# Two more steps of lag in a windowed-attention pipeline, and a second PSUM buffer in a mixture-of-experts stage

## The chip, the cores and the metric

The kernel runs on the 8 cores of one Trainium2 chip. Each core computes 2048 of the 16384 tokens, with its own copy of all weights. The metric is the device time in microseconds of the slowest core.

## What is computed

One transformer layer, cut to its core:

```python
# x: [16384, 1024]; every block ends with layernorm(x + block(x))
q, k, v = split(x @ qkv_w + qkv_b)              # 16 heads of 64
s = (q / 8) @ k.T                               # local window: the 128 keys before a query
local = softmax(where(0 < dist <= 128, s, -1e9)) @ v
pooled = x.reshape(64, 256, 1024).mean(1)       # 64 latent tokens over ALL 16384 tokens
rk, rv = split(pooled @ rkv_w)
remote = softmax(where(chunk_allowed, (x @ rq_w) @ rk.T / 8, -1e9)) @ rv @ rout_w
gate = sigmoid(local @ gl_w + remote @ gr_w)
x = layernorm(x + (gate*local + (1-gate)*remote) @ out_w)
# FFN: shared part plus 16 experts, the 4 chosen ones weighted by `combine`
shared = (silu(x @ sgw.T) * (x @ suw.T)) @ sdw.T
for e in range(16):                             # dense: all tokens through all experts
    h = silu(x @ gate_w[e]) * (x @ up_w[e])     # [tokens, 256]
    routed += (h * combine[:, e]) @ down_w[e]
x = layernorm(x + shared + routed)
```

## The kernel before

The program is a row of blocks (phases 0, 1, 15, 2, 3). Inside a block each engine has its own queue, in the order in which the Python code calls `P.op`; an engine works its queue strictly in order. `waits` are semaphore values of other engines, and `P.drain("ve")` stands between dependent VectorE operations. The blocks follow one another with a barrier.

**Phase 0** works through the core's 2048 tokens in four chunks of 512. For each chunk: TensorE transposes the tokens (L334, through `transpose_group`), ScalarE copies them out (`xfm`, L341), then follow the q, k, v and rq projections (L350, through `proj`), then `emit_pool(8)`, then the attention loop. A group is one pair of heads and 128 queries; there are G = 32 groups in a chunk, 128 in all. A group passes six stages:

- `stA`: TensorE scores into `ps_sc` (L494). It waits for the newest `stB`.
- `stB`: VectorE adds the mask (two operations, L511) into `maskedb`, takes the row maximum (L519) and clamps it (L523). `maskedb` has two buffers; it waits for `stC` of the group two before.
- `stC`: ScalarE exponentials (two operations with a sum, L538) into `p_b`, two buffers.
- `stD`: VectorE adds an epsilon to the sum (L553), inverts it (L558) and scales the row (two operations, L565) into `pn_b`, two buffers.
- `stE`: TensorE transposes the four 128x128 parts (L581) into one of two `ps_bt`; ScalarE copies them to `pT_b` (L591).
- `stG`: TensorE multiplies with v (four matmuls, L611) into one of two `ps_pr`; ScalarE casts the result into `local_sb` (L622).

After every eighth group TensorE gets six tiles of the pooling of all 16384 tokens (`emit_pool(6)`, L319, 12 matmuls), whose loads (`ring`) are issued on the GpSimd queue. At the end of a chunk SyncE stores `local_sb`. The next chunk's transposes use the same `ps_bt` slots, and stand behind the loop in TensorE's queue. After the last chunk the pooled tokens are evacuated, transposed and projected, and the block ends with the store of `local_sb`.

**Phase 2** runs the experts: 8 token blocks of 256, 16 experts each, 128 steps. In TensorE's order a step is: the combine weights of this expert broadcast to 128 partitions (`ps_wb`, L1442, one matmul), 16 gate matmuls into `ps_g` (L1453), 16 up matmuls into `ps_u` (L1466), and the 8 down matmuls of the previous expert into `ps_rt` (L1489), which collect over the 16 experts. ScalarE applies Silu to `ps_g` (L1504). VectorE multiplies it with `ps_u` (`h_sb`, L1508) and that with `ps_wb` (`hwst`, L1518). The up matmuls wait for the load of `uwb` and for the previous expert's `h_sb`. Loads: `uwb` on SyncE's queue, `dwb` on GpSimd's, four buffers each. At the end of a token block VectorE adds the residual (`ry`, L1536), with a load of `y1r` and a store per half on SyncE's queue, ahead of the next block's `uwb` loads.

PSUM in phase 2: `ps_rt` two tiles of 1024 f32 columns, `ps_g` and `ps_u` one of 512 each, `ps_wb` two of 256.

Of the kernel before, what the change touches and what calls it, by code (L numbers as in the profile page):

```python
# [7 lines left out]
F32 = mybir.dt.float32  # L8
# [103 lines left out]
class Builder:  # L112
# [88 lines left out]
    def phase0(self):  # L201
        nc, d, sm = self.nc, self.d, self.sem
        pe, pp, ve, se = (sm[k] for k in ("pe", "pp", "ve", "se"))
        c0 = ExitStack()
        S = lambda n, s, t: c0.enter_context(nc.sbuf_tensor(n, s, t))
        PS = lambda n, s, t: c0.enter_context(nc.psum_tensor(n, s, t))
# [36 lines left out]
        P = Plan()  # L243
# [27 lines left out]
        for dst, src in [(self.maskAB[:], d["maskAB_in"]),  # L271
# [14 lines left out]
             waits=[self.tk_consts], inc=se)  # L286
# [79 lines left out]
        for c in range(self.p0_nch):  # L366
# [14 lines left out]
            if c + 1 < NCH:  # L381
                ld_own[c + 1] = st_xo.dma(
                    P, "ge", xown[:], R3(d["x_own"][(c + 1) * 512:(c + 2) * 512, :]),
                    waits=[(pe, tr_pe)])
# [241 lines left out]

            ST = self.p0_st
            if self.p0_attn:
                for i in range(G + 3):
                    if 1 <= i <= G and ST >= 2:  # L630
                        stB(i - 1)
                    if i < G:
                        stA(i)
                    if 1 <= i <= G and ST >= 3:
                        stC(i - 1)
                    if 2 <= i <= G + 1 and ST >= 4:
                        stD(i - 2)
                    if 2 <= i <= G + 1 and ST >= 5:
                        stE(i - 2)
                    if 3 <= i <= G + 2 and ST >= 6:  # L640
                        stG(i - 3)
                    if i < G and i % 8 == 7:
                        emit_pool(6)

# [723 lines left out]
    def phase2(self):  # L1368
# [12 lines left out]
        ry = S("ry", [128, 2, 1024], F32)  # L1381
        ps_rt = [PS(f"ps_rt{i}", [128, 1024], F32) for i in range(2)]
        ps_g = PS("ps_g2", [128, 512], F32)
        ps_u = PS("ps_u2", [128, 512], F32)
        ps_wb = [PS(f"ps_wb{i}", [128, 256], F32) for i in range(2)]

        P = Plan()
        st_y1s = self.new_stream("y1s2", 4)
# [7 lines left out]
        y1r_rel = [None, None]  # L1396
        ry_rel = [None, None]
        wb_rel = [None, None]
        rt_rel = [None, None]
        silu_prev = 0  # L1400
        h_prev = 0
# [17 lines left out]
        for tb in range(8):  # L1419
# [8 lines left out]
            for e_i in range(17):  # L1428
                if e_i < 16:
                    su = e_i % 4  # L1430
                    wu = [uwb_rel[su]] if uwb_rel[su] is not None else []
                    uwld[e_i] = st_uw.dma(P, "sy", uwb[:, su],
                                          d["uwbf_sp"][e_i],
                                          waits=wu + self.tk_precast_ud)
                    wd = [dwb_rel[su]] if dwb_rel[su] is not None else []
                    dwld[e_i] = st_dw.dma(P, "ge", dwb[:, su], d["dwbf_sp"][e_i],
                                          waits=wd + self.tk_precast_ud)
                    sw = e_i % 2
                    if self.p2_mode >= 1:
                        ww = [wb_rel[sw]] if wb_rel[sw] is not None else []  # L1440
                        ww += [(se, self._p15_comb_se), self.tk_gec]
                        P.op("te", lambda e, sw=sw, e_i=e_i, tb=tb: e.matmul(  # L1442
                            ps_wb[sw][:], self.ue16[:, e_i * 128:(e_i + 1) * 128],
                            self.combT[0:16, tb * 256:(tb + 1) * 256],
                            start=True, stop=True), waits=ww, inc=pe)
                    vwb = pe.n
                    if self.p2_mode < 2:
                        continue
                    wg = [self.tk_gw, ldy_a, ldy_b, (se, silu_prev)]
                    for mh in range(2):  # L1450
                        for cc in range(8):
                            P.op("te", lambda e, e_i=e_i, cc=cc, mh=mh, sl=sl:
                                 e.matmul(ps_g[:, mh * 256:(mh + 1) * 256],  # L1453
                                          self.gw_sb[:, e_i, cc,
                                                     mh * 128:(mh + 1) * 128],
                                          y1s[:, sl, cc, :],
                                          start=(cc == 0), stop=(cc == 7)),
                                 waits=wg if (cc == 0 and mh == 0) else (),
                                 inc=pe if (cc == 7 and mh == 1) else None)
                            wg = ()  # L1460
                    vg = pe.n
                    wu2 = [uwld[e_i], (ve, h_prev)]
                    for mh in range(2):
                        for cc in range(8):
                            P.op("te", lambda e, su=su, cc=cc, mh=mh, sl=sl:
                                 e.matmul(ps_u[:, mh * 256:(mh + 1) * 256],  # L1466
                                          uwb[:, su, cc, mh * 128:(mh + 1) * 128],
                                          y1s[:, sl, cc, :],
                                          start=(cc == 0), stop=(cc == 7)),
                                 waits=wu2 if (cc == 0 and mh == 0) else (),  # L1470
                                 inc=pe if (cc == 7 and mh == 1) else None)
                            wu2 = ()
                    vu = pe.n
                    uwb_rel[su] = (pe, pe.n)
# [27 lines left out]
                if e_i < 16:  # L1502
                    sgsl = e_i % 2
                    P.op("se", lambda e, sgsl=sgsl: e.activation(  # L1504
                        out=sg_sb[:, sgsl, :], in_=ps_g[:], func=AF.Silu),
                        waits=[(pe, vg), (ve, h_prev2[sgsl])], inc=se)
                    silu_prev = se.n
                    P.op("ve", lambda e, sgsl=sgsl: e.tensor_tensor(  # L1508
                        out=h_sb[:], in0=sg_sb[:, sgsl, :], in1=ps_u[:],
                        op=OP.mult),  # L1510
                        waits=[(se, silu_prev), (pe, vu)], inc=ve)
                    h_prev = ve.n
                    h_prev2[sgsl] = ve.n
                    P.drain("ve")
                    sw = e_i % 2
                    wb3 = ps_wb[sw][:].unsqueeze(1).broadcast_to([128, 2, 256])
                    whw = [(pe, prev_down_pe)]
                    P.op("ve", lambda e, e_i=e_i, wb3=wb3: e.tensor_tensor(  # L1518
                        out=hwst[:, e_i % 2, :].rearrange("p (n m) -> p n m", n=2),
                        in0=h_sb[:].rearrange("p (n m) -> p n m", n=2),  # L1520
                        in1=wb3, op=OP.mult), waits=whw, inc=ve)
                    hw_ve[e_i] = ve.n
                    wb_rel[sw] = (ve, ve.n)
                    P.drain("ve")
                    prev_down_pe = down_pe[e_i - 1] if e_i >= 1 else prev_down_pe
# [391 lines left out]
```

How the kernel before makes its waits and increments, by code:

```python
        def run(e, fn=fn, w=tuple(w), inc=inc, incn=incn):  # L66
            for (s, v) in w:
                e.wait_ge(s.h, v)
            ins = fn(e)
            if inc is not None:
                ins.then_inc(inc.h, incn)
```

## Time and profile before

| | us |
|---|---|
| median of the two runs shown | 2845.77 |
| lowest and highest of them | 2769.34, 2922.2 |
| profiled execution | 2742.85 |
| its span, slowest core (core 4) | 2741.3 |
| spans of the eight cores | 2712.7 to 2741.3 |

Over the span TensorE is busy 62%, its weight loads 39%, VectorE 30%, ScalarE 23%, GpSimd 7%. These are averages over stages with different limits: phase 0 takes about the first 696 us, phases 1 and 15 run to about 1396, the experts to about 2265, and the shared part to the end. A stretch's limit is read from the order of time inside it: the engine whose queue has no gap but those it makes itself.

### The profile page before, as it was taken

The page shows a single profiled execution, that of the slowest core. Times are in us where ns is not written, and L with a number is a line of the kernel's source. Part 1 is how long each engine was busy: PE and PEld are TensorE (multiplying, and loading weights), DVE is VectorE, ACT ScalarE, POOL GpSimd, SP SyncE. Part 2 cuts the span into 40 slices and gives each one's busy share as a digit, 9 for nine tenths or more (in the row PEclk, how much of TensorE's full clock was granted, in tenths as well). Part 3 has the DMA queues.
Part 4 walks back from the last instruction along what each step waited for, and adds up shares of the span by engine and source line. Part 5 has one row for each costly group of instructions (what it writes and reads, how often), then busy time and mean ns, then how long its engine had stood idle before and what let it go on. Part 6 is the DMA issues. An engine that isn't in the chain of part 4 may idle for free. (4 is left out here: it accounts for less than half of the span.)

```text
span 2741.3 us, 33324 instructions; the slowest of 8 cores (2712.7 to 2741.3 us)
## 1 busy us (share of the span) xinstructions
PE 1712.0 (62%) x11255; PEld 1055.7 (39%) x11368; DVE 819.1 (30%) x2083; ACT 642.6 (23%) x1693; POOL 201.9 (7%) x329
## 2 busy tenths in 40 slices
PE   0858677685345442000249779779779783877886
PEld 0423233332111110000136557557556553655654
DVE  0173645638344441001232222222222220222222
ACT  1264554636312220002611001001000000122212
POOL 1100100000011111110001000000000000000000
PEclk9968777686666666555569899889899896998998
DMA  9644553523977777656735655555555546122112
GB/s 169 100 70 73 72 83 54 78 39 55 151 164 177 153 169 145 137 130 171 210 130 170 198 182 175 191 181 185 177 179 196 171 139 215 55 77 85 55 62 77
DMA packets 185652, 363.15 MB, mean 132 GB/s; under 512 B 30272, under 2 KB 89984, under 8 KB 183952
## 3 DMA queue, kind: packets, MB, share of 16 engines
q0 software_dynamic: 94048, 182.90, 32.9%
q1 hardware_dynamic: 91440, 178.11, 20.3%
q8 instruction: 96, 1.57, 0.2%
q14 instruction: 68, 0.56, 0.1%
HBM read 367.69 MB, written 79.69 MB: 163 GB/s over the span
## 5 line engine op out<-in xcount | busy, mean ns | idle before, releaser
L1466 PE MATMUL ps_u<-y1s,uwb 128*128 128x256 bf16 x2048 | 257.5, 281 | 114.8 <-DMA uwb<-uwbf_sp 114.8
L1508 DVE TENSOR_TENSOR h_sb<-sg_sb,ps_u 128x512 bf16<-128x512 bf16 x128 | 88.0, 688 | 585.5 <-PE ps_u L1466 585.5
L1466 PEld LDWEIGHTS ps_u<-y1s,uwb 128*128 128x128 bf16 x2048 | 205.5, 101 | 146.0 <-issue 117.0
L1453 PE MATMUL ps_g<-y1s,gw_sb 128*128 128x256 bf16 x2048 | 250.7, 277 | 9.9 <-DMA y1s<-y1fm_sp 9.9
L1504 ACT ACTIVATE sg_sb<-ps_g 128x512 bf16<-128x512 f32 x128 | 76.4, 597 | 759.6 <-PE ps_g L1453 759.6
L1489 PE MATMUL ps_rt<-dwb,hwst 128*128 128x512 bf16 x960 | 228.1, 379 | 4.5 <-DVE hwst L1518 0.5
L1636 PE MATMUL ps_g<-y1s,sgw 128*128 128x256 bf16 x1024 | 144.5, 288 | 114.5 <-ACT sgs L1652 61.1
L1453 PEld LDWEIGHTS ps_g<-y1s,gw_sb 128*128 128x128 bf16 x2048 | 192.1, 99 | 48.9 <-issue 11.7
L1170 PE MATMUL ps_b<-ident,y1bf 128*128 128x128 bf16 x128 | 16.2, 306 | 277.7 <-ACT y1bf L1150 229.1
L1636 PEld LDWEIGHTS ps_g<-y1s,sgw 128*128 128x128 bf16 x1024 | 104.7, 103 | 134.6 <-issue 116.7
L538 ACT ACTIVATE p_b<-maskedb,mn_sb 128x256 bf16<-128x256 f32 x256 | 127.9, 500 | 58.0 <-DVE mn_sb L523 58.0
L1645 PE MATMUL ps_u<-y1s,suw 128*128 128x256 bf16 x1024 | 140.6, 283 | 0.0
L1489 PEld LDWEIGHTS ps_rt<-dwb,hwst 128*128 128x128 bf16 x1024 | 99.5, 98 | 98.3 <-issue 4.9
L45 POOL DMA_DIRECT2D dwb<-dwbf_sp x128 | 67.6, 529 | 896.6 <-PE ps_wb L1442 730.7
L1657 DVE TENSOR_TENSOR h_sb<-sgs,ps_u 128x256 bf16<-128x256 bf16 x128 | 53.3, 421 | 237.0 <-PE ps_u L1645 166.2
L350 PE MATMUL ps_pr<-xfm,qkvw 128*128 128x512 bf16 x500 | 117.7, 397 | 6.1 <-ACT xfm L341 5.4
L1170 PEld LDWEIGHTS ps_b<-ident,y1bf 128*128 128x128 bf16 x128 | 12.4, 137 | 279.1 <-issue 279.1
L1675 PE MATMUL ps_d<-sdw,h_sb 128*128 128x512 bf16 x496 | 109.6, 379 | 8.0 <-DVE h_sb L1657 7.5
L1645 PEld LDWEIGHTS ps_u<-y1s,suw 128*128 128x128 bf16 x1024 | 104.5, 102 | 16.1
L511 DVE TENSOR_TENSOR maskedb<-ps_sc,maskAB 128x256 f32<-128x256 f32 x240 | 90.1, 418 | 55.7 <-PE ps_sc L494 55.5
L581 PE MATMUL ps_bt<-ident,pn_b 128*128 128x128 bf16 x512 | 68.8, 281 | 60.5 <-DVE pn_b L565 60.5
L591 ACT COPY pT_b<-ps_bt 128x512 bf16<-128x512 bf16 x128 | 75.0, 586 | 105.0 <-PE ps_bt L581 105.0
(181 smaller groups left out, 2020.8 us busy)
## 6 DMA issues: line engine op xcount, KB each, us to landing
dwb<-dwbf_sp POOLq DMA_DIRECT2D x128, 512.0 KB, 4.0
uwb<-uwbf_sp SPq DMA_DIRECT2D x128, 512.0 KB, 3.9
ring<-x_all POOLq DMA_DIRECT2D x64, 512.0 KB, 10.2
xres<-x_own SPq DMA_DIRECT2D x16, 512.0 KB, 17.2
gw_sb<-gate_w POOLq DMA_DIRECT2D x4, 2048.0 KB, 40.1
stg<-down_w POOLq DMA_DIRECT2D x16, 512.0 KB, 6.4
y_sp<-y0b SPq DMA_DIRECT2D x16, 512.0 KB, 5.8
dwbf_sp<-stg POOLq DMA_DIRECT2D x16, 512.0 KB, 3.0
```

The lines of the kernel that those rows point to most:

```text
L350: P.op("te", lambda e, sl=slot, kk=kk, nc2=ncols, nr=nrows: e.matmul(ps_pr[sl][0:nr, 0:nc2], lhs_fn(kk), rhs_fn(kk), start=(kk == 0), stop ...
L511: e.tensor_tensor(out=maskedb[:, mb, hh * 256:(hh + 1) * 256], in0=ps_sc[hh][:, mb * 256:mb * 256 + 256], in1=m, op=OP.add),
L538: P.op("se", lambda e, mb=mb, hh=hh, f=f: e.activation(out=p_b[:, mb, hh * 256:(hh + 1) * 256], in_=maskedb[:, mb, hh * 256:(hh + 1) * 256 ...
L591: P.op("se", lambda e, sl=slot, mb=mb: e.copy(out=pT_b[:, mb, :], in_=ps_bt[sl][:]), waits=wv, inc=se)
L1453: e.matmul(ps_g[:, mh * 256:(mh + 1) * 256], self.gw_sb[:, e_i, cc, mh * 128:(mh + 1) * 128], y1s[:, sl, cc, :], start=(cc == 0), stop=(cc ...
L1466: e.matmul(ps_u[:, mh * 256:(mh + 1) * 256], uwb[:, su, cc, mh * 128:(mh + 1) * 128], y1s[:, sl, cc, :], start=(cc == 0), stop=(cc == 7)),
L1489: nh=nh, first=first, last=last: e.matmul(ps_rt[mt][:, nh * 512:(nh + 1) * 512], hwst[:, ep % 2, kc * 256 + mt * 128: kc * 256 + mt * 128 ...
L1504: P.op("se", lambda e, sgsl=sgsl: e.activation(out=sg_sb[:, sgsl, :], in_=ps_g[:], func=AF.Silu), waits=[(pe, vg), (ve, h_prev2[sgsl])], i ...
L1508: P.op("ve", lambda e, sgsl=sgsl: e.tensor_tensor(out=h_sb[:], in0=sg_sb[:, sgsl, :], in1=ps_u[:], op=OP.mult), waits=[(se, silu_prev), (p ...
L1636: P.op("te", lambda e, sl2=slg, mh=mh, cc=cc, sl=sl: e.matmul(ps_g[sl2][:, 0:256], sgw[:, cc, mh * 128:(mh + 1) * 128], y1s[:, sl, cc, :], ...
L1645: P.op("te", lambda e, sl2=slu, mh=mh, cc=cc, sl=sl: e.matmul(ps_u[sl2][:, 0:256], suw[:, cc, mh * 128:(mh + 1) * 128], y1s[:, sl, cc, :], ...
L1675: last=last, sld=sld: e.matmul(ps_d[sld][:, nh * 512:(nh + 1) * 512], h_sb[:, kc, mt * 128:(mt + 1) * 128], sdw[:, kc, nh * 512:(nh + 1) * ...
```

## The change

Two independent edits.

In the attention loop the stages from `stC` on are issued later: exponentials of group i-2 instead of i-1 in step i, normalisation of i-3 instead of i-2, transposes of i-4 instead of i-2, value products of i-5 instead of i-3. The loop has two more steps to finish. No stage's own code changes; no buffer is added.

In phase 2 `ps_u` gets a second buffer, used in turn, so that the up matmuls wait for the product of two experts before instead of the previous one. The PSUM for it comes from `ps_wb`, which has one buffer now. A new ScalarE copy, ahead of the Silu in ScalarE's queue, brings `ps_wb` into `wb_sb` in SBUF (f32, two buffers), and VectorE's second product reads it there. The next `ps_wb` matmul waits for that copy; the copy waits for the second product of two experts before.

```diff
-                for i in range(G + 3):
+                for i in range(G + 5):
                     if 1 <= i <= G and ST >= 2:
                         stB(i - 1)
                     if i < G:
                         stA(i)
-                    if 1 <= i <= G and ST >= 3:
-                        stC(i - 1)
-                    if 2 <= i <= G + 1 and ST >= 4:
-                        stD(i - 2)
-                    if 2 <= i <= G + 1 and ST >= 5:
-                        stE(i - 2)
-                    if 3 <= i <= G + 2 and ST >= 6:
-                        stG(i - 3)
+                    if 2 <= i <= G + 1 and ST >= 3:
+                        stC(i - 2)
+                    if 3 <= i <= G + 2 and ST >= 4:
+                        stD(i - 3)
+                    if 4 <= i <= G + 3 and ST >= 5:
+                        stE(i - 4)
+                    if 5 <= i <= G + 4 and ST >= 6:
+                        stG(i - 5)
                     if i < G and i % 8 == 7:
                         emit_pool(6)
...
-        ps_u = PS("ps_u2", [128, 512], F32)
-        ps_wb = [PS(f"ps_wb{i}", [128, 256], F32) for i in range(2)]
+        ps_u = [PS(f"ps_u2{i}", [128, 512], F32) for i in range(2)]
+        ps_wb = PS("ps_wb", [128, 256], F32)
+        wb_sb = S("wb_sb", [128, 2, 256], F32)
...
-                        ww = [wb_rel[sw]] if wb_rel[sw] is not None else []
-                        ww += [(se, self._p15_comb_se), self.tk_gec]
+                        ww = [(se, self._p15_comb_se), self.tk_gec]
+                        if wb_ps_rel[0] is not None:
+                            ww.append(wb_ps_rel[0])
...
+                        vwb = pe.n
+                        wwc = [(pe, vwb)]
+                        if wb_rel[sw] is not None:
+                            wwc.append(wb_rel[sw])
+                        P.op("se", lambda e, sw=sw: e.copy(
+                            out=wb_sb[:, sw, :], in_=ps_wb[:]), waits=wwc,
+                            inc=se)
+                        wb_ps_rel[0] = (se, se.n)
...
-                    wu2 = [uwld[e_i], (ve, h_prev)]
+                    su2 = e_i % 2
+                    wu2 = [uwld[e_i]]
+                    if psu_rel[su2] is not None:
+                        wu2.append(psu_rel[su2])
...
+                    psu_rel[su2] = (ve, ve.n)
...
-                    wb3 = ps_wb[sw][:].unsqueeze(1).broadcast_to([128, 2, 256])
-                    whw = [(pe, prev_down_pe)]
+                    wb3 = wb_sb[:, sw, :].unsqueeze(1).broadcast_to([128, 2, 256])
+                    whw = [(pe, prev_down_pe), (se, silu_prev)]
```

## Rows read from the trace of the kernel before

**Rows 1.** Busy by stretch (attention; experts): length, PE, PEld, DVE, ACT, POOL, clock, DMA.

```profile
130.47:226.80 96.33, 54.69 (x366) 26.60 (x365) 73.58 (x256) 57.40 (x187) 8.42 (x13) 0.61 0.51 72
1396.30:2265.00 868.70, 726.79 (x5184) 508.84 (x5248) 195.57 (x272) 77.70 (x129) 67.62 (x128) 0.92 0.55 180
```

**Rows 2.** Order of time, one attention group: start us, us, engine, line, operation, [idle before].

```profile
188.88 0.51 ACT L538 ACTIVATE p_b<-maskedb,mn_sb 128x256 bf16<-128x256 f32 x1 [0.18 <-DVE mn_sb L523]
188.94 0.40 PE L494 MATMUL ps_sc<-k_sb,q_sb 64*128 64x256 bf16 x2 [0.72 <-DVE mn_sb L523]
...
189.21 0.48 DVE L565 TENSOR_SCALAR pn_b<-p_b,rvv 128x256 bf16<-128x256 bf16 x2
...
189.61 0.75 DVE L511 TENSOR_TENSOR maskedb<-ps_sc,maskAB 128x256 f32<-128x256 f32 x2
189.79 0.19 ACT L538 ACTIVATION_READ_ACCUMULATOR p_b<-maskedb,mn_sb 128x1 f32 x1
...
189.84 0.59 PE L581 MATMUL ps_bt<-ident,pn_b 128*128 128x128 bf16 x4 [0.51 <-DVE pn_b L565]
...
190.43 0.69 DVE L519 TENSOR_REDUCE mn_sb<-maskedb 128x2 f32<-128x512 f32 x1
190.52 0.58 ACT L591 COPY pT_b<-ps_bt 128x512 bf16<-128x512 bf16 x1 [0.54 <-PE ps_bt L581]
...
191.19 0.17 DVE L523 TENSOR_SCALAR mn_sb<-mn_sb 128x2 f32<-128x2 f32 x1
...
191.51 0.40 PE L494 MATMUL ps_sc<-k_sb,q_sb 64*128 64x256 bf16 x2 [0.72 <-DVE mn_sb L523]
```

**Rows 3.** Waits of the whole run: who waited for whom, us in total, times, longest.

```profile
DVE maskedb L511 <- PE ps_sc L494: 62.6, 20, 6.6
```

**Rows 4.** Order of time in the expert stage, one expert.

```profile
1445.56 0.69 DVE L1508 TENSOR_TENSOR h_sb<-sg_sb,ps_u 128x512 bf16<-128x512 bf16 x1 [4.07 <-PE ps_u L1466]
1446.34 0.69 DVE L1518 TENSOR_TENSOR hwst<-h_sb,ps_wb 128x512 bf16<-128x512 bf16 x1
...
1447.11 0.28 PE L1442 MATMUL ps_wb<-combT,ue 16*128 16x256 bf16 x1
...
1449.08 1.91 PE L1466 MATMUL ps_u<-y1s,uwb 128*128 128x256 bf16 x16
...
1451.10 0.69 DVE L1508 TENSOR_TENSOR h_sb<-sg_sb,ps_u 128x512 bf16<-128x512 bf16 x1 [4.07 <-PE ps_u L1466]
```

**Rows 5.** Waits of TensorE in the expert stage, 1420 to 2240 us.

```profile
PE ps_u L1466 <- DMA uwb<-uwbf_sp: 109.9, 7, 16.7
```

**Rows 6.** Order of time on VectorE at the start of the first chunk's loop.

```profile
130.87 0.76 DVE L511 TENSOR_TENSOR maskedb<-ps_sc,maskA0B 128x256 f32<-128x256 f32 x2 [6.56 <-PE ps_sc L494]
133.18 0.76 DVE L511 TENSOR_TENSOR maskedb<-ps_sc,maskA0B 128x256 f32<-128x256 f32 x2 [0.55 <-PE ps_sc L494]
135.77 0.75 DVE L511 TENSOR_TENSOR maskedb<-ps_sc,maskA0B 128x256 f32<-128x256 f32 x2
```

**Rows 7.** Order of time at the end of the first chunk's loop.

```profile
222.45 4.41 PE L319 MATMUL ps_pool<-ring,zpool 128*64 128x512 bf16 x12
...
227.29 0.58 ACT L591 COPY pT_b<-ps_bt 128x512 bf16<-128x512 bf16 x1 [2.85 <-PE ps_bt L581]
...
227.77 0.27 ACT L622 CAST local_sb<-ps_pr 128x128 bf16<-128x128 f32 x1
227.93 0.60 ACT L591 COPY pT_b<-ps_bt 128x512 bf16<-128x512 bf16 x1
...
228.67 0.31 PE L611 MATMUL ps_pr<-pT_b,v_sb 128*64 128x128 bf16 x4 [0.35 <-ACT pT_b L591]
228.91 0.62 PE L334 MATMUL ps_bt<-ident,xown 128*128 128x128 bf16 x8
```

**Rows 8.** Groups of instructions by line and shape: busy, mean ns, idle before.

```profile
L1504 ACT ACTIVATE sg_sb<-ps_g 128x512 bf16<-128x512 f32 x128 | 76.4, 597 | 759.6 <-PE ps_g L1453 759.6
...
L974 DVE TENSOR_TENSOR d_bf<-localre,remote 128x512 bf16<-128x512 bf16 x32 | 13.6, 426 | 47.8 <-PE ps_g L968 43.3 <-issue 4.5
```

More of the change, by code:

```diff
@@ L1398, in phase2 @@
         wb_rel = [None, None]
+        wb_ps_rel = [None]
+        psu_rel = [None, None]
         rt_rel = [None, None]
@@ L1439, in phase2 @@
                     if self.p2_mode >= 1:
-                        ww = [wb_rel[sw]] if wb_rel[sw] is not None else []
-                        ww += [(se, self._p15_comb_se), self.tk_gec]
-                        P.op("te", lambda e, sw=sw, e_i=e_i, tb=tb: e.matmul(
-                            ps_wb[sw][:], self.ue16[:, e_i * 128:(e_i + 1) * 128],
+                        ww = [(se, self._p15_comb_se), self.tk_gec]
+                        if wb_ps_rel[0] is not None:
+                            ww.append(wb_ps_rel[0])
+                        P.op("te", lambda e, e_i=e_i, tb=tb: e.matmul(
+                            ps_wb[:], self.ue16[:, e_i * 128:(e_i + 1) * 128],
                             self.combT[0:16, tb * 256:(tb + 1) * 256],
                             start=True, stop=True), waits=ww, inc=pe)
-                    vwb = pe.n
+                        vwb = pe.n
[6 more added lines that the diff above has]
+                        wb_ps_rel[0] = (se, se.n)
                     if self.p2_mode < 2:
@@ L1461, in phase2 @@
                     vg = pe.n
-                    wu2 = [uwld[e_i], (ve, h_prev)]
+                    su2 = e_i % 2
+                    wu2 = [uwld[e_i]]
+                    if psu_rel[su2] is not None:
+                        wu2.append(psu_rel[su2])
                     for mh in range(2):
                         for cc in range(8):
-                            P.op("te", lambda e, su=su, cc=cc, mh=mh, sl=sl:
-                                 e.matmul(ps_u[:, mh * 256:(mh + 1) * 256],
+                            P.op("te", lambda e, su=su, su2=su2, cc=cc, mh=mh,
+                                 sl=sl:
+                                 e.matmul(ps_u[su2][:, mh * 256:(mh + 1) * 256],
                                           uwb[:, su, cc, mh * 128:(mh + 1) * 128],
@@ L1507, in phase2 @@
                     silu_prev = se.n
-                    P.op("ve", lambda e, sgsl=sgsl: e.tensor_tensor(
-                        out=h_sb[:], in0=sg_sb[:, sgsl, :], in1=ps_u[:],
+                    P.op("ve", lambda e, sgsl=sgsl, su2=su2: e.tensor_tensor(
+                        out=h_sb[:], in0=sg_sb[:, sgsl, :], in1=ps_u[su2][:],
                         op=OP.mult),
```

## The prediction

> **What bounds the kernel now.** I read the spans of the cores first (2712.7 to 2741.3 us, clocks 0.787 to 0.791: no core stands out), then busy time by stretch, then the order of time inside the two stretches that the diff touches, then the waits. The two edits lie in an attention loop of 32 groups that runs four times, 96.33 us in the first chunk, and in the expert stage, 868.70 us [rows 1].
>
> In the attention stretch no engine looks full: VectorE 73.58 of 96.33 us, ScalarE 57.40, TensorE 54.69 at a granted clock of 0.61, the lower level for most of it. The order of time says more [rows 2]. TensorE's scores (L494) start at 188.94 and again at 191.51, so a group takes 2.57 us. In it VectorE runs without a break: normalisation (L565) 189.21 to 189.69, mask adds (L511) 189.61 to 190.36, row maximum (L519) 190.43 to 191.12, clamp (L523) 191.19 to 191.36, and then the small operations of the next normalisation. The gaps of 0.07 us follow its own drains. None of its rows shows idle time before it. So VectorE's queue sets the 2.57 us; TensorE and ScalarE wait for it, and their idle time there costs nothing. VectorE itself waits where pooling matmuls (L319) stand ahead of the next scores, and at the start of a chunk: 20 times in the whole run, 62.6 us [rows 3].
>
> In the expert stage the order of time shows TensorE as the bound [rows 4]: the `ps_wb` matmul starts at 1447.11 and the up matmuls at 1449.08, with only the 16 gate matmuls between them, and weight loads and matmuls together leave little of the stage free. VectorE's read of `ps_u` (L1508) runs 1445.56 to 1446.25, and the next write of `ps_u` starts at 1449.08. In the waits of 820 us of this stage the longest of TensorE's is 109.9 us for `uwb` loads, seven times at a block boundary, and there is none for VectorE on `ps_u` [rows 5].
>
> **Attention: what the new order moves.** Today step i issues mask+max(i-1), scores(i), exp(i-1), normalise(i-2), transpose(i-2), value product(i-3). Afterwards the last four are exp(i-2), normalise(i-3), transpose(i-4), value product(i-5). Counts of instructions, tiles and DMAs stay; 32 groups end two steps later.
>
> Steady state: VectorE has the same eight operations per group, and none waited for data that now comes earlier. scores(i) still waits for mask+max(i-1), the newest VectorE result, and mask+max(i) still waits for scores(i): 188.94 to 189.61, hidden under the normalisation, as before. I cost the steady state at 0. Its bound on the good side is the drain gaps: period 2.57 less VectorE's durations (0.75+0.69+0.17+0.17+0.17+0.48 = 2.43, two of the 0.17 being the normalisation's small steps, sized as the clamp) is 0.14 us, 18 us over 128 groups.
>
> Fill: normalisation starts one step later, so one more step runs without it. Such a step took 2.31 us (130.87, [0.55] us idle, 133.18), a step with it 2.59 (133.18 to 135.77) [rows 6]: 0.28 us gained per chunk.
>
> Tail: now it counts, since the next chunk's transposes queue behind it on TensorE and ScalarE. Before, the last pooling block ends at 222.45+4.41 = 226.86; two transposes and three value products are left behind it, and the next chunk's transposes start at 228.91, 2.05 us later [rows 7]. Afterwards four transposes and five value products are left, and exp(31) too, because ScalarE's queue has the copy of transpose(28) ahead of it, which waits for the pooling block. Counting from the block's end with steps from rows: first copy starts at 0.43 (227.29); cast 0.48 later, 0.91; exp(31) 0.16 later (227.77 to 227.93), 1.07, and lasts 1.10 (188.88 to 189.98 [rows 2]), 2.17; copy(29) to 2.75; its value product on TensorE ends at about 3.1 (0.31). Meanwhile VectorE normalises 31 after exp(31), 0.17+0.17+0.48 with gaps, 0.97 us (2.57 less 1.60 for adds to clamp), done near 3.2. transpose(31) starts at 3.3 and its copy 0.5 later, 3.8; from a last copy to the last value product 0.74 (227.93 to 228.67) and on to the next transposes 0.24: 4.8. Less 2.05: 2.75 us per chunk. The fourth chunk's tail delays the pooled projections and the spill that phase 1 waits for, by about as much. Sum: 4 x (2.75 - 0.28) = 9.9 us, taken as +10. Bounds: +4, if ScalarE's work packs better (0.48+0.16 us for each of two extra pairs, less the fill, 1.0 per chunk); +16, if exp(31), copies and normalisation run strictly one after another (four copies 0.58, five casts 0.27, exp 1.10, normalisation 0.97, 5.7 us, plus the 0.43 and 0.24, less 2.05, is 4.3 per chunk).
>
> **Experts: a second `ps_u`, `ps_wb` copied out.** The wait taken off TensorE, up(e+1) on h(e), had been met 2.83 us before it was reached (1446.25 against 1449.08) [rows 4]: 0 us. If it had just been uncovered it would be worth up to one VectorE read, 0.69.
> The Trainium skill, "Perfetto Trace Analysis", section Matmuls, says that independent matmul groups should rotate through different PSUM banks so that one's evacuation overlaps the next one's matmuls. By that rule alone the 88 us of rival (e) would come back; the trace disagrees, since the gate, down and `ps_wb` matmuls already lie between two uses of `ps_u`.
>
> Added are 128 ScalarE copies of 128x256 f32. The trace has none; the nearest are the cast of 128x128 at 0.27 us and the Silu of 128x512 at 0.60 [rows 7, 8], so 0.27 to 0.60 and I take 0.43, 35 to 77 us in all. ScalarE is busy 77.70 of 868.70 us there [rows 1]. Behind a copy on its queue stands silu(e), which waits for gate(e) and so for 1.9 us longer than the copy's source. The new wait, `ps_wb`(e+1) on copy(e), has a period of 5.54 us (1445.56+5.54 is the next h) to be met; it costs 0. Without that cover it would be 0.43 x 128 = 55 us. The product `hwst` (L1518, 0.69) now reads SBUF: between the all-SBUF bf16 add's 0.43 [rows 8] and, on the bad side, 0.26 more than now; it lies off the path except before the last down matmuls of a block, eight times, so -2 to +2 us, taken as 0. SP's and POOL's queues issue the same loads on the same waits.
> The Trainium skill, "VectorE: DVE Perf Modes", section Rules for kernel authors, says to accept the slower PSUM read, or copy to SBUF first if many operations follow. One operation reads `wb_sb`, so the rule speaks against the edit; the idle ScalarE makes it cost nothing, and the sum is the same.
>
> **The sum** is made on the profiled execution: 2742.85 + 10 + 0 = 2753 us. The median of the two runs shown is 2845.77 (2769.34 and 2922.2), 3.8% above the profiled time; I forecast on the profiled time's scale.
>
> **Rivals.** (a) *Only the tail grows*: 2753. For it: no idle time on VectorE and TensorE to recover. Chance 0.66.
> (b) *The tail lets TensorE's clock fall before the next projection.* Four transposes take 0.59 at the low level [rows 2] and half of 0.62 for eight at the start of the next chunk [rows 7]; eight such groups in four chunks are 32 x 0.28 = 9 us more: 2762. Against: the clock in the attention stretch is low already. Chance 0.12.
> (c) *VectorE's gaps shrink* because its semaphore waits are all met early: -18+10, 2735. Against: the gaps follow drains. Chance 0.08.
> (d) *The two-deep buffers bind.* exp(i-1) frees `maskedb` for mask(i+1). It now runs after copy(i-4) and cast(i-5), which follow scores(i): 188.94 + 0.40 + 0.68 + 0.48 + 0.27 + 1.10 = 191.87 [rows 2, 7], and VectorE wants the buffer at 189.61+2.57 = 192.18. Before, exp ended at 189.98; the slack falls from 2.2 to 0.3 us. The loop spans two groups, so every 0.1 us beyond the slack costs 0.05 us x 128 = 6 us. A chain 1.3 us longer than these rows say gives 128 x 0.5 = 64 us: 2817. It is the mechanism on the slower side, and passes 2% from a chain 1.15 us longer. Chance 0.08, most of it over 2%.
> (e) *The waits paid off after all*, because VectorE no longer stands still behind the pooling blocks (all of the 62.6 us of [rows 3]: 2753 - 63 = 2690), or because the read of `ps_u` really lay open in every expert (128 x 0.69 = 88: 2665). Against: the scores behind a pooling block keep their place in TensorE's queue, and TensorE never waited for VectorE on `ps_u` [rows 5]. Chance 0.04, most of it over 2%.
> (f) *`ps_wb`'s single buffer stops TensorE* each expert: 2753 + 55 = 2808. Against: 5 us of slack. Chance 0.02.
>
> **How the numbers follow.** Likeliest 2753; its own bounds give 2743 to 2765 (+4-2 and +16+2, with half a per mille for repeat runs). The range takes in (b) and (c) and reaches up to (d) and (f), and covers that the lowest timed run lies 27 us above the profiled one: 2735 to 2820. What a measurement of this kernel can tell from no change is about 2%, 55 us: faster 0.03 (most of (e)), slower 0.08 (most of (d), and (f), which lies at the bound), same 0.89.
>
> **What would show it.** Right: scores of neighbouring groups still 2.57 us apart; the time from the last pooling block's end to the next chunk's transposes near 4.8 instead of 2.05; ScalarE's `wb_sb` copies near 0.43 us and no TensorE wait for them; the expert period still 5.54. Wrong: a period of groups below 2.5 (c) or above 2.65 with VectorE waiting for ScalarE at L511 (d); an expert period that moves; or VectorE's wait behind the pooling blocks shrinking (e).

## The result, and the profile after

The changed kernel takes 2753.37 us (median of 43 runs, 2743.6 the lowest). The kernel before, run beside it, takes 2743.18 us (42 runs, 2730.95 the lowest). The ratio is 1.0036, 95% interval 1.0025 to 1.0047: slower by about 10 us, which is within 2% and yet far outside the uncertainty of so many runs. The median of two runs shown ahead of the prediction, 2845.77 us, was 3.7% above what more runs give for the same kernel. Some executions of either kernel run a few per cent longer with the cores of one die at a lower clock; the ratio leaves them out, as by its size it does the 2922.2 us shown there.

Span and mean granted TensorE clock of the slowest core in the profiled execution after (the others take 2725.8 to 2745.8 us; before 2712.7 to 2741.3):

```profile
core 7: 2750.5 us, clock 0.783
```

One steady attention group of the changed kernel, in order of time (start us, us, engine, line, operation, [idle before it and what ended it]); it answers to [rows 2]:

```profile
188.67 0.17 DVE L523 TENSOR_SCALAR mn_sb<-mn_sb 128x2 f32<-128x2 f32 x1
...
188.98 0.17 DVE L558 RECIPROCAL rvv<-rvv 128x2 f32<-128x2 f32 x1
188.99 0.40 PE L494 MATMUL ps_sc<-k_sb,q_sb 64*128 64x256 bf16 x2 [1.31 <-DVE mn_sb L523]
189.29 0.48 DVE L565 TENSOR_SCALAR pn_b<-p_b,rvv 128x256 bf16<-128x256 bf16 x2
...
189.69 0.75 DVE L511 TENSOR_TENSOR maskedb<-ps_sc,maskAB 128x256 f32<-128x256 f32 x2
...
191.59 0.40 PE L494 MATMUL ps_sc<-k_sb,q_sb 64*128 64x256 bf16 x2 [1.31 <-DVE mn_sb L523]
```

VectorE still works without a break, and TensorE and ScalarE still wait for it. But the scores are now 2.60 us apart (188.99 to 191.59), not 2.57, and between the reciprocal's end (188.98+0.17 = 189.15) and the scaling (189.29) lie 0.14 us, where the kernel before has 0.07.

The end of the first chunk, answering to [rows 7]:

```profile
222.13 4.70 PE L319 MATMUL ps_pool<-ring,zpool 128*64 128x512 bf16 x12
...
227.25 0.59 ACT L591 COPY pT_b<-ps_bt 128x512 bf16<-128x512 bf16 x1 [3.43 <-PE ps_bt L581]
227.27 0.48 DVE L565 TENSOR_SCALAR pn_b<-p_b,rvv 128x256 bf16<-128x256 bf16 x2 [2.50 <-PE ps_bt L581]
...
227.89 0.52 ACT L538 ACTIVATE p_b<-maskedb,mn_sb 128x256 bf16<-128x256 f32 x1
...
229.10 0.17 DVE L553 TENSOR_SCALAR rvv<-ssum 128x2 f32<-128x2 f32 x1 [1.35 <-ACT p_b L538]
...
229.65 0.48 DVE L565 TENSOR_SCALAR pn_b<-p_b,rvv 128x256 bf16<-128x256 bf16 x2
...
230.76 0.59 ACT L591 COPY pT_b<-ps_bt 128x512 bf16<-128x512 bf16 x1 [0.47 <-PE ps_bt L581]
...
231.49 0.30 PE L611 MATMUL ps_pr<-pT_b,v_sb 128*64 128x128 bf16 x4 [0.59 <-ACT pT_b L591]
231.72 0.62 PE L334 MATMUL ps_bt<-ident,xown 128*128 128x128 bf16 x8
```

The last pooling block ends at 222.13+4.70 = 226.83, and the next chunk's transposes start at 231.72. This stretch, called the tail below, takes 4.89 us, against 2.05. The chain is the one of the prediction: copy(28) at 227.25, exp(31) at 227.89, its end lets VectorE invert the sum at 229.10, scaling at 229.65, transpose, copy at 230.76, value product at 231.49.

The expert stage after: the groups of the new copy, the second product and the up matmuls (count | busy us, mean ns of one | idle before and what ended it):

```profile
L1454 ACT COPY wb_sb<-ps_wb 128x256 f32<-128x256 f32 x128 | 47.8, 373 | 530.4 <-PE ps_wb L1446 530.4
L1534 DVE TENSOR_TENSOR hwst<-h_sb,wb_sb 128x512 bf16<-128x512 bf16 x128 | 88.6, 692 | 12.1 <-issue 0.4
L1481 PE MATMUL ps_u<-y1s,uwb 128*128 128x256 bf16 x2048 | 257.2, 281 | 117.1 <-DMA uwb<-uwbf_sp 117.1
```

The 128 copies take 0.37 us each, `hwst` takes 0.69 us as before, the expert period is still 5.54 us (`h_sb` at 1456.35 and 1461.89), and TensorE waits there for the same thing as before, the `uwb` loads (117.1 us over the whole stage, against 114.8 before; [rows 5] has 109.9 of them).

From the first scores of a chunk to the next transposes (in the fourth chunk: to those of the pooled tokens), called the loop below, the slowest cores take:

| us | chunk 1 | 2 | 3 | 4 |
|---|---|---|---|---|
| before (core 4) | 98.44 | 96.55 | 96.69 | 96.50 |
| after (core 7) | 101.06 | 99.45 | 99.32 | 99.23 |

The sum is 10.9 us more. From the transposes to the next chunk's first scores it is 57.03 before and 57.6 after, three times: 1.8 us more. The transposes of the pooled tokens, which follow the fourth loop, so start 12.9 us later (702.64 against 689.73), and the first expert matmul 11.6 us later (1407.87 against 1396.28). One core against another carries some chance with it; averaged over the eight cores these two delays are 12.6 and 11.3 us, and the spans are 10.6 us longer. What lies between the two points takes a little over 1 us back.

### The profile page after: what moved, and what is told of

Same layout as the page of the kernel before. It is cut to its first block and busy times, and to the rows that moved or that the text cites. A ratio compares the mean times of both kernels' runs of the same rounds, so it can differ in the third digit from the quotient of the medians.

```text
span 2750.5 us, 33823 instructions; the slowest of 8 cores (2725.8 to 2750.5 us)
## 1 busy us (share of the span) xinstructions
PE 1721.7 (63%) x11368; PEld 1056.6 (38%) x11368; DVE 814.8 (30%) x2083; ACT 680.8 (25%) x1821; POOL 201.8 (7%) x329
## 5 line engine op out<-in xcount | busy, mean ns | idle before, releaser
L1481 PE MATMUL ps_u<-y1s,uwb 128*128 128x256 bf16 x2048 | 257.2, 281 | 117.1 <-DMA uwb<-uwbf_sp 117.1
L1504 PE MATMUL ps_rt<-dwb,hwst 128*128 128x512 bf16 x1024 | 241.9, 379 | 1.1 <-issue 0.5
L1454 ACT COPY wb_sb<-ps_wb 128x256 f32<-128x256 f32 x128 | 47.8, 373 | 530.4 <-PE ps_wb L1446 530.4
L494 PE MATMUL ps_sc<-k_sb,q_sb 64*128 64x256 bf16 (+1 forms) x256 | 44.4, 330 | 121.5 <-DVE mn_sb L523 121.5
```

Of the source, the lines that this page charges most:

```text
L1481: e.matmul(ps_u[su2][:, mh * 256:(mh + 1) * 256], uwb[:, su, cc, mh * 128:(mh + 1) * 128], y1s[:, sl, cc, :], start=(cc == 0), stop=(cc == ...
L1504: nh=nh, first=first, last=last: e.matmul(ps_rt[mt][:, nh * 512:(nh + 1) * 512], hwst[:, ep % 2, kc * 256 + mt * 128: kc * 256 + mt * 128 ...
```

## The experiments

**Each edit alone.** The first kernel has only the loop's new order, the second only the second `ps_u` with the `wb_sb` copy.

```diff
 # attention only: kernel before, with
-                for i in range(G + 3):
+                for i in range(G + 5):
 ...                                       # and the later stC, stD, stE, stG
 # experts only: the changed kernel, with
-                for i in range(G + 5):
+                for i in range(G + 3):
 ...                                       # and the old order
```

> Only the attention loop's new order; the expert stage as before. Theory (the whole loss lies in the loop's tail and its clock): ratio to the kernel before 1.0036, about +10 us; last pooling block to the next chunk's transposes 4.9 us instead of 2.05, group period 2.60. Rival (the expert edit shares in the loss): ratio 1.001 to 1.002.

> Only the second ps_u and the copied ps_wb; the attention loop as before. Theory: ratio 1.000 within 0.001, expert period 5.54 us, TensorE never waiting for the copy. Rival (the expert edit pays, but the attention edit hides it): ratio 0.998 or less. Rival (it costs): 1.002 or more.

The attention edit alone gave 1.0043 (1.0016 to 1.0071): loops of 100.5, 99.4, 99.3 and 99.2 us on its slowest core, tail 4.89. The expert edit alone gave 1.0005 (0.9983 to 1.0027): loops as before, tail 2.05. So the loss comes from the loop's order; what the expert edit costs or brings is too small for these runs, less than 0.3% either way.

**What lengthened the steady group.** `P.op`, the helper that puts an operation into an engine's queue, leaves out a wait when the engine has already waited for that value of the semaphore or a later one. Before, normalise(g) asks for transpose(g-2), and VectorE had already waited for the scores that were issued after it: the wait was dropped. Afterwards transpose(g-2) is issued after scores(g+2), the newest that VectorE has waited for, so the wait stays in the program. It is met long before it is reached: in the changed kernel the transposes of 186.71 end at 187.32, and the scaling that waits for them starts at 189.29. A third `pn_b` buffer makes normalise(g) ask for transpose(g-3), and the wait is dropped again:

```diff
-        pn_b = S("pn_b", [128, 2, 512], BF16)
+        pn_b = S("pn_b", [128, 3, 512], BF16)
-        rel_pn = [None, None]
+        rel_pn = [None, None, None]
 ...                                       # pn_b and rel_pn indexed by g % 3
```

> The changed kernel with three buffers for the normalised rows pn_b instead of two, so that normalise(g) waits for the transposes of g-3, not g-2. Theory: the 0.03 us by which the group period grew (2.575 to 2.605) is the semaphore wait that normalise(g) now has on transpose(g-2), which is issued after the scores that VectorE has waited for already; with three buffers the period returns to 2.575 and about 3 us come back, ratio to before 1.0025; the tail stays at 4.9 us, since exp(31) sets it and not normalise(30), which waits for the pooling block in the changed kernel. Rival (the period grew for another reason, such as operand traffic of ScalarE): period stays at 2.605. Rival (normalise(30) behind the pooling block sets the tail): tail falls to about 4 us.

The order of time in this kernel:

```profile
187.53 0.17 DVE L558 RECIPROCAL rvv<-rvv 128x2 f32<-128x2 f32 x1
187.53 0.40 PE L494 MATMUL ps_sc<-k_sb,q_sb 64*128 64x256 bf16 x2 [1.25 <-DVE mn_sb L523]
187.78 0.48 DVE L565 TENSOR_SCALAR pn_b<-p_b,rvv 128x256 bf16<-128x256 bf16 x2
...
190.07 0.40 PE L494 MATMUL ps_sc<-k_sb,q_sb 64*128 64x256 bf16 x2 [1.25 <-DVE mn_sb L523]
```

The gap ahead of the scaling is back to 0.08 us (187.70 to 187.78), and the group takes 2.54 us. It is even shorter than before the change, because with the longer lag the wait of normalise(g) on exp(g) is dropped too: VectorE has already waited for exp(g) in order to reuse `maskedb`. The kernel as a whole did not follow: 1.0052 (1.0034 to 1.0070), where 1.0025 was expected. The pooling matmuls show where the gain went; the groups of L319 in phase 0, before, after and with three buffers (mean ns of one is the last number before the second bar):

```profile
L319 PE MATMUL ps_pool<-ring,zpool 128*64 128x512 bf16 x243 | 79.9, 498 | 0.0
```

```profile
L319 PE MATMUL ps_pool<-ring,zpool 128*64 128x512 bf16 x244 | 86.6, 528 | 0.0
```

```profile
L319 PE MATMUL ps_pool<-ring,zpool 128*64 128x512 bf16 x252 | 93.3, 547 | 0.0
```

The program has 256 of them (some records are missing). They are the same instructions; the granted clock of TensorE beside them is lower. The granted clock of the second chunk's loop and of the projections behind it (us, PE busy, clock, DMA share, GB/s), before, after and with three buffers:

```profile
285.94:382.49 96.55, 54.39 (x385) 0.65 0.52 74
382.49:439.52 57.03, 53.30 (x254) 0.94 0.39 61
```

```profile
289.38:388.83 99.45, 53.72 (x386) 0.64 0.56 76
388.83:446.44 57.61, 54.85 (x259) 0.91 0.31 54
```

```profile
290.98:390.18 99.20, 55.92 (x385) 0.61 0.52 78
390.18:448.02 57.84, 55.30 (x258) 0.90 0.25 50
```

With three buffers the saving, 0.065 us x 28 undisturbed groups x 4 = 7 us, is met by 0.019 us x 256 = 4.9 us of slower pooling matmuls, 0.3 x 4 = 1.3 us of a longer tail (5.21 where 4.9 was expected: its last four transposes take 0.59 us instead of 0.38, at a granted clock of 0.50) and 0.2 x 3 = 0.6 us of slower transposes behind it. The mechanism of the wait is shown; that this saving always draws the clock down is not.

**Half the lag.** Exponentials and normalisation keep their old steps, transposes and value products run one step later (i-3, i-4) with the loop one step longer.

```diff
-                    if 2 <= i <= G + 1 and ST >= 5:
-                        stE(i - 2)
-                    if 3 <= i <= G + 2 and ST >= 6:
-                        stG(i - 3)
+                    if 3 <= i <= G + 2 and ST >= 5:
+                        stE(i - 3)
+                    if 4 <= i <= G + 3 and ST >= 6:
+                        stG(i - 4)
```

> The changed kernel, but in the attention loop exponentials and normalisation keep the old lag (i-1, i-2) and only transposes and value products are one step later (i-3, i-4). Theory 1 (the tail is what the work left behind the last pooling block costs, and exp(31) is then done inside the block): last pooling block's end to next chunk's transposes 2.7 to 3.1 us, between 2.05 and 4.9. Theory 2 (a semaphore wait in VectorE's queue costs time even when it is met long before): normalise(g) still waits for exp(g) and now also for the transposes of g-2, so the group period is 2.63 to 2.65 us, above both kernels (2.575 and 2.605). Ratio to before 1.002 to 1.005. Rival (only waits that are not met cost time): period 2.575 or less.

The tail is 2.84 us and the scores of neighbouring groups are 2.645 us apart (two neighbours here, 2.65; 319.81 to 327.75 is three periods):

```profile
325.10 0.39 PE L494 MATMUL ps_sc<-k_sb,q_sb 64*128 64x256 bf16 x2 [1.35 <-DVE mn_sb L523]
327.75 0.40 PE L494 MATMUL ps_sc<-k_sb,q_sb 64*128 64x256 bf16 x2 [1.35 <-DVE mn_sb L523]
```

That completes a table of four kernels, in which VectorE's operations are the same and only the two waits of the normalisation, both met early, differ:

| period of a group, us | wait on exp(g) dropped | wait on exp(g) kept |
|---|---|---|
| wait on transpose dropped | 2.54 (three `pn_b`) | 2.575 (before) |
| wait on transpose kept | 2.605 (after) | 2.645 (half the lag) |

The wait on the transpose costs 0.065 to 0.07 us per group, the one on exp(g) 0.035 to 0.04, in both rows and both columns. The time also appears where the wait stands: the wait on the transpose lies between the reciprocal and the scaling, and from start to start it is 0.24 us there where that wait is dropped and 0.31 where it is kept; from the clamp to the first operation of the normalisation 0.08 us without and 0.11 with the wait on exp(g). The whole kernel came to 1.0009 (0.9996 to 1.0021), where 1.002 to 1.005 was expected: a chunk's loop grew by only 0.15 to 0.27 us in chunks 2 to 4, since here too the pooling blocks start earlier, which the expectation left out (below).

**The tail.** In the changed kernel the last six pooling tiles are given out one per step, from step 31 to 36, instead of all six in step 31.

```diff
-                    if i < G and i % 8 == 7:
+                    if i < G - 1 and i % 8 == 7:
                         emit_pool(6)
+                    elif i in (31, 32, 33, 34, 35, 36):
+                        emit_pool(1)
```

> The changed kernel with the last six pooling tiles of a chunk spread over the last six steps (31 to 36), so that TensorE has them between the pieces of the tail; same work. Theory (the tail behind the block is where the loss lies): from scores(31) to the next chunk's transposes about 7 us instead of 9.5, 10 us come back, ratio to before 0.999 to 1.001. Rival (the loss lies in the steps or in the clock): ratio stays at 1.003 or above.

The ratio is 0.9998 (0.9985 to 1.0010): nearly all of the 0.36% is gone. From the last scores to the next transposes it takes 8.2 us, against 10.7 in the changed kernel and 8.1 in the one before; about 7 had been expected. The end of the first chunk in this kernel:

```profile
229.03 0.59 PE L319 MATMUL ps_pool<-ring,zpool 128*64 128x512 bf16 x2
...
229.89 0.59 PE L319 MATMUL ps_pool<-ring,zpool 128*64 128x512 bf16 x2
230.42 0.62 PE L334 MATMUL ps_bt<-ident,xown 128*128 128x128 bf16 x8
231.82 0.38 PE L334 MATMUL ps_bt<-ident,xown 128*128 128x128 bf16 x4 [0.79 <-ACT xfm L341]
```

The pooling matmuls now fill the time between the tail's transposes and value products. They run at 0.29 us each there, and the next chunk's transposes at 0.38 us for four. In the changed kernel the same transposes ran at the lower clock:

```profile
231.72 0.62 PE L334 MATMUL ps_bt<-ident,xown 128*128 128x128 bf16 x8
233.14 1.27 PE L334 MATMUL ps_bt<-ident,xown 128*128 128x128 bf16 x8 [0.79 <-ACT xfm L341]
234.74 1.27 PE L334 MATMUL ps_bt<-ident,xown 128*128 128x128 bf16 x8 [0.33 <-ACT xfm L341]
```

1.27 us for eight is 0.64 for four, against 0.38. From 226.8 to 231.7, the tail, TensorE was busy 2.70 of 4.90 us at a granted clock of 1.00; from 233.1 to 238.0 the clock is 0.50. In the kernel before, the transposes slow down too, but 4.2 us after the first of them and not 1.4. The granted clock over the first 11.1 us of the transposes, before, after, and with the tail covered:

```profile
228.90:240.00 11.10, 7.58 (x47) 0.69 1.03 184
```

```profile
231.70:242.80 11.10, 8.34 (x46) 0.55 0.72 150
```

```profile
230.40:241.50 11.10, 7.96 (x46) 0.69 0.90 185
```

From there to the next scores the covered kernel needs 57.02 us, as before, and the changed one 57.66. So the last pooling block, put ahead of the tail in one piece, costs twice: the tail's chain has nothing beside it (2.85 us), and the clock falls earlier in what follows (0.6 us).

**Room for the pooling tiles.** If the lag has a use, it should be where TensorE's queue is disturbed. Both orders were tried with one pooling tile in three of four steps (24 tiles in 32 steps, as many as before) in place of four blocks of six.

```diff
-                    if i < G and i % 8 == 7:
-                        emit_pool(6)
+                    if i < G and i % 4 != 3:
+                        emit_pool(1)
```

> The changed kernel with the pooling tiles issued one in each of three steps out of four, instead of six after every eighth step; same work. Theory: VectorE's stand-still behind the pooling blocks (about 3.2 us, 12 times) and the part of the last block that nothing covers (about 3 us, 4 times) are what the loop can still lose, and TensorE has room for one tile per group: 45 to 50 us less, ratio to before 0.985 to 0.988. Rival (the ring loads then bind, or a tile delays the scores in each group): ratio 0.995 to 1.01.

> The kernel before with the pooling tiles one in each of three steps out of four, as e4 has them in the changed one. It tells whether the longer lag is what makes room for the tile. Theory: in the old order value products end late in a step (190.8 of a step whose next scores are due at 191.5), and a tile of 0.86 to 1.06 us delays the scores in those steps by 0.2 to 0.5 us; loop about 91 to 93 us against 89.0 in e4, less the shorter tail, ratio to before 0.985 to 0.992. Rival (the lag makes no room): loop below 88 us, ratio 0.984 or less.

On the changed kernel the ratio is 0.9897 (0.9868 to 0.9925), 41 us below its own 2753.37 where 45 to 50 were expected; on the kernel before it is 0.9870 (0.9834 to 0.9907). The loops take 89.1 and 86.8 us. The old order with tiles in it:

```profile
320.00 0.39 PE L494 MATMUL ps_sc<-k_sb,q_sb 64*128 64x256 bf16 x2
321.58 1.06 PE L319 MATMUL ps_pool<-ring,zpool 128*64 128x512 bf16 x2
322.57 0.40 PE L494 MATMUL ps_sc<-k_sb,q_sb 64*128 64x256 bf16 x2
```

The scores stay 2.57 us apart with a tile in the step. The expectation that the old order has no room (91 to 93 us) fell: 1.06 us of pooling fit into TensorE's idle time without any lag, and the lag only adds 2.0 to 2.3 us per chunk. (The ratio lies inside the range expected with that theory; the loop is what refutes it.)

**The expert stage's real wait.** The wait that the change removed was never waited for; the one that was is `uwb` at a block boundary. Here it is in the kernel before:

```profile
1504.70 1.22 DVE L1536 TENSOR_TENSOR ry<-ps_rt,y1r 128x1024 f32<-128x1024 f32 x1 [2.31 <-PE ps_rt L1489]
...
1506.38 0.42 SPq L45 DMA_DIRECT2D y1r<-y_sp  x1
1512.64 1.22 DVE L1536 TENSOR_TENSOR ry<-ps_rt,y1r 128x1024 f32<-128x1024 f32 x1 [6.71 <-DMA y1r<-y_sp]
1513.94 0.32 SPq L45 DMA_DIRECT2D routedy_sp<-ry  x1
...
1515.75 14.54 SPq L45 DMA_DIRECT2D uwb<-uwbf_sp  x6
...
1522.40 3.57 PE L1466 MATMUL ps_u<-y1s,uwb 128*128 128x256 bf16 x16 [15.81 <-DMA uwb<-uwbf_sp]
```

The first weight load of the new block is issued at 1515.75, because in SyncE's queue it stands behind two stores of `ry` and the second `y1r` load, and these wait for VectorE. TensorE stands still for 15.81 us, and its 16 up matmuls then take 3.57 us instead of 1.91: the granted clock is 1.00 in the 31 us up to 1506 and 0.50 from 1522.4 to 1526.0. The edit issues, at the end of a block, both `y1r` loads first, then the next block's four `uwb` loads, then the stores:

```diff
+            for mt in range(2):
+                ldy1s.append(st_y1r.dma(P, "sy", y1r[:, mt, :],
+                                        d["y1_sp"][tb * 2 + mt], waits=wy))
+            for e_n in (range(4) if tb + 1 < 8 else []):
+                uw_pre[(tb + 1, e_n)] = st_uw.dma(
+                    P, "sy", uwb[:, e_n], d["uwbf_sp"][e_n],
+                    waits=[uwb_rel[e_n]])
             for mt in range(2):
-                ldy1 = st_y1r.dma(...)
+                ldy1 = ldy1s[mt]
```

> The kernel before with only the order of SyncE's queue changed at the end of a token block in the expert stage: both y1r loads, then the first four uwb loads of the next block, then the two stores that wait for VectorE. Theory (the expert stage's open wait is the uwb load behind those stores, not ps_u): TensorE's waits for uwb fall from 115 us to under 15, 90 to 105 us less, ratio to before 0.962 to 0.968. Rival (the loads then collide, or the wait moves to ry or dwb): ratio above 0.98.

The ratio is 0.9521 (0.9493 to 0.9550), more than expected. The same boundary:

```profile
1495.98 2.35 DVE L1547 TENSOR_TENSOR ry<-ps_rt,y1r 128x1024 f32<-128x1024 f32 x2 [2.32 <-PE ps_rt L1493]
...
1497.27 1.45 SPq L45 DMA_DIRECT2D routedy_sp<-ry  x2
...
1497.70 1.91 PE L1470 MATMUL ps_u<-y1s,uwb 128*128 128x256 bf16 x16
```

The up matmuls start 1.7 us after the start of the residual sums, at a granted clock of 1.00. TensorE's waits for `uwb` fall from 114.8 to 4.1 us, and the slow matmuls behind them, 1.66 us at a boundary, are gone, which the expectation had not counted. VectorE's wait for the second `y1r` is gone too; it lay inside the same standstill and is not to be added. A boundary saves 129/7 = 18 us.

**Both together.** The spread tiles and SyncE's new order, on the kernel before and on the changed kernel (the two diffs above).

> The kernel before (lag i-1, single ps_u) with both the pooling tile in three of four steps and the new order on SyncE's queue at a block boundary. The two gains lie in different stages and should add: 38 us (e7) and 129 us (e8) off the time of before, ratio near 0.939, 0.935 to 0.943. Rival: TensorE's clock gives part back once both stretches are denser, ratio 0.945 or more. Loops of the attention stage stay near 87 us, waits for uwb near 4 us.

> The changed kernel (both edits) with the same two additions. If the lag's price is the longer tail (2.2 us per chunk in the spread form, from the loops of 89.0 and 86.8 us), this is 9 us above the same additions on the kernel before: ratio near 0.942 and 0.003 above the other run. Rival: in the spread form the longer lag gives room to the TensorE queue and pays: the ratio is the other run's or below it. Loops near 89 us.

On the kernel before: 0.9371 (0.9321 to 0.9421), 2568.55 us. On the changed one: 0.9402 (0.9361 to 0.9443), 2576.80 us, with loops of 88.8 to 89.2 against 86.7 to 87.1 us. The gains add, as expected. The four loops of the changed kernel are 8.7 us longer together (356.2 against 347.5), most of it the tail (about 8.4 against 6.55 us behind the last tile; 1.3 us more in the first chunk, 1.85 in the others), and the medians are 8.3 us apart. By their intervals alone the two ratios are not told apart; but five of the six executions of the changed kernel take longer than 2571.11 us, the longest of the five of the other that entered its ratio. The best version does without the change.

## Why the prediction was right or wrong

**The sum and its place: the number right, two steps around it wrong.** The sum gave +10 us on the profiled 2742.85 us, a ratio of 1.0036; measured are 1.0036 and 2753.37 us against 2743.18. That the number came out so closely is in part luck: it rests on a tail sized rightly and on three terms it lacked, which nearly cancel (below). Two steps around it failed. First, the forecast of 2753 us stood 3.3% below the 2845.77 us given as the time before, and the text left both numbers standing: it took the profiled execution as the scale without saying that the two runs' median must then be too high, so that its own number, read against the median, says faster while its mechanism says slower. Secondly, the step "about what a measurement of this kernel can tell from no change" took 2% for it. 43 runs against 42 tell 0.11% apart, and against that measure a sum of +0.36% with bounds of +4 and +16 us was a forecast of slower, not of the same. The bounds of the likeliest case had one sign, and the chances should have been drawn from it.

**Steady state, costed at 0: wrong, +0.03 us.** "VectorE has the same eight operations per group" held, and that none waited held too. What failed is that a wait which is met costs nothing: the change turned a dropped wait into a kept one and a kept one into a dropped one, +0.065 and -0.035 us. Over 28 undisturbed groups a chunk that is 0.84 us, 3.4 us in all. The 0.14 us that the prediction called the drain gaps is also not their sum: in [rows 2] the mask adds start at 189.61, before the scaling ends at 189.69, so there are four gaps of 0.07 us and operations that overlap by as much as makes up the rest. These gaps stayed, to 0.01 us, in all four kernels, except where a wait stands in one. The 0.035 us that three buffers took off each group (128 x 0.035 = 4.5 us, where rival (c) had 18) lie between the clamp and the start of the normalisation, where the kernel has no drain.

**Fill, -0.28 per chunk: near**, -0.22 to -0.24 in chunks 2 and 3 (2.59 to 2.37 us for the step, 7.47 to 7.23 for the first three). In the first chunk, where [rows 6] were read, the three steps took 7.86 us before and 7.69 after, in the fourth 7.82 and 7.22; single steps that are 0.3 to 0.4 us longer, for which the profile shows no cause, occur there.

**Tail, +2.75: right**, measured +2.84 to +2.87, on all eight cores. One link was missed: normalise(30) waits 2.50 us for transpose(28), which stands behind the pooling block. It did not matter, since exp(31) ends later: with three `pn_b` that wait is gone, and the normalisation of group 31 still starts 2.27 us behind the block.

**The pooling blocks: left out, twice.** With the lag the transposes and value products ahead of a block no longer wait for VectorE, so a block starts 0.38 us after its mask add instead of 0.96 (308.05 against 307.67, before 305.43 against 304.47). The first block of the second chunk, before and after:

```profile
304.47 0.75 DVE L511 TENSOR_TENSOR maskedb<-ps_sc,maskAB 128x256 f32<-128x256 f32 x2
...
305.43 3.89 PE L319 MATMUL ps_pool<-ring,zpool 128*64 128x512 bf16 x12
```

```profile
307.67 0.75 DVE L511 TENSOR_TENSOR maskedb<-ps_sc,maskAB 128x256 f32<-128x256 f32 x2
...
308.05 4.41 PE L319 MATMUL ps_pool<-ring,zpool 128*64 128x512 bf16 x12
```

What stands behind it, the next scores or at the end the tail, comes 0.6 us earlier, four times a chunk: -2.4 us. This is a small part of rival (e), which had the gain lie in VectorE's stall. And the blocks run slower: in the second chunk 4.41, 4.46, 4.66 and 4.61 us against 3.89, 4.05, 4.30 and 4.43, +1.5 us. The sum for that chunk is 2.85 + 0.84 + 1.5 - 2.4 - 0.24 = 2.55 us of the 2.90 measured; 0.3 us of the rest is one step of 2.83 us instead of 2.54 (VectorE idle before 299.85, for nothing that the profile shows), which chunks 3 and 4, 2.63 and 2.73 us longer, do not have. The forecast of 2.47 per chunk was near because three terms it lacked, +0.84, +1.5 and -2.4, nearly cancel: that is luck.

**Rival (b), the clock falls before the next projection: it happened**, in a smaller size. It costs 0.6 us three times and not 9 us; the covered tail brings it back. Its argument against, that the clock is low already, was wrong: in the kernel before the transposes of 230.32 to 232.8 ran at the higher level, four in 0.38 us (granted clock 0.93 from 230.3 to 233.0).

**Rivals (c), (d), (f): not seen.** VectorE's wait for TensorE's scores at L511 is 63.3 us after, against the 62.6 of [rows 3], and it waits for ScalarE nowhere at L511: the two-deep buffers hold and the slack of 0.3 us sufficed. No engine waits for the single `ps_wb` to come free.

**Experts, 0: right.** The copy took 0.37 us (0.43 taken, between 0.27 and 0.60). `hwst` took 0.692 us against 0.687: neither end of -2 to +2 us was reached. The Trainium skill, "VectorE: DVE Perf Modes", section What auto-detection actually checks, says that the faster mode for 16-bit data is taken if every tensor is 16-bit and read element by element in steps of one; `wb_sb` is f32. The trace agrees (0.692 us), and the better end of that term, drawn from an add with three bf16 tensors [rows 8], could have been left out.

## What to carry to other kernels

Before lengthening a software pipeline, ask which engine waits for a late stage in the steady state; if none does, the longer lag mainly adds its length to every place where the pipeline runs empty, so cover that place with independent work or leave the lag alone. A wait that the profile never shows as idle time is not worth PSUM or SBUF; the ones at the boundaries (here a weight load queued behind stores that wait for VectorE) were worth 4.8%. When a forecast and a small sample of times disagree by more than the effect, say which of them is off before saying faster or slower.

## What the runs showed of the hardware that was not expected

- **A wait that is already met is not free on VectorE.** In a queue without idle time it added 0.065 to 0.07 us (on TensorE's semaphore) and 0.035 to 0.04 us (on ScalarE's) per group, in four kernels whose VectorE operations are the same. Why the two differ is open: one stands behind a drain, the other does not.
- **A faster VectorE queue went with a slower TensorE.** With three `pn_b` buffers the groups come faster, and yet the granted clock of the second chunk fell from 0.64 to 0.61 and the pooling matmuls went from 528 to 547 ns. With the tiles spread (loop 86.8 us, clock 0.53) they took 561 ns, and the kernel gained all the same, since VectorE's queue sets the time.
- **A stalled TensorE pays twice.** Behind the 15.81 us wait the 16 up matmuls took 3.57 us instead of 1.91, at a granted clock of 0.50 instead of 1.00.
- **The order within one issuing queue was the largest cost that any experiment here removed.** Loads that were ready stood behind stores that were not, and putting them first in the same queue took 4.8% off. The Trainium skill, "Perfetto Trace Analysis", section DMA Optimizations, says that it may make sense, in loops above all, to give input and output transfers to different issuing engines. No run here tried that.
